# Moving the tiles that two neighbouring blocks share in a gather-and-sum kernel on one Trainium2 core

## The reference

```
x = x + GIN(layernorm(x))          # two sums over edges, four products, relu
x = x + slice_attention(layernorm(x))
x = x + GCN(layernorm(x))          # one sum over edges, weighted by degree
x = x + mixture_of_experts(layernorm(x))   # top 2 of 8 experts
```

## Time and profile before

| | us |
|---|---|
| median of 3 runs | 4030.41 |
| lowest and highest | 4024.98, 4033.82 |
| the profiled execution | 4029.44 |
| its span, first to last instruction | 4027.3 |

### The profile page before, as it was taken

One profiled execution on the slowest core, in us unless ns is written; L12 is line 12 of the kernel. 1 busy time (PEld: TensorE's weight loads), 2 busy tenths in 40 slices (PEclk: granted clock), 3 DMA queues, 4 the chain that ended last, 5 costly groups with the idle time before them and its releaser, 6 DMA issues. The chain is left out here.

```text
span 4027.3 us, 40958 instructions
## 1 busy us (share of the span) xinstructions
PE 3255.7 (81%) x12396; PEld 2172.8 (54%) x12396; DVE 1552.6 (39%) x5917; ACT 496.3 (12%) x1159; POOL 2691.4 (67%) x2719
## 2 busy tenths in 40 slices
PE   3688888888967999999999876567667666769996
PEld 2455555555543555555555464445455554558885
DVE  7422232222213445444444444345454444532221
ACT  3111111111100001010001011000000000023332
POOL 3777777777746777777777403777777777626664
PEclk7899999999988999999999988888888898879998
DMA  6444454444559777777776447444444444438887
GB/s 212 112 130 130 131 149 138 130 130 131 152 154 344 221 219 211 210 215 226 226 212 200 133 139 239 128 141 130 143 132 130 140 130 140 123 111 201 204 202 184
DMA packets 326339, 678.01 MB, mean 168 GB/s; under 512 B 60274, under 2 KB 156886, under 8 KB 325850
## 3 DMA queue, kind: packets, MB, share of 16 engines
q0 software_dynamic: 163376, 455.13, 41.0%
q10 hardware_dynamic: 93460, 117.75, 8.7%
q1 hardware_dynamic: 69290, 102.51, 7.8%
HBM read 582.15 MB, written 100.31 MB: 169 GB/s over the span
## 5 line engine op out<-in xcount | busy, mean ns | idle before, releaser
L292 POOL DMA_INDIRECT s_edge_rows<-table,w_src_idx x2421 | 2383.8, 985 | 796.0 <-issue 704.2
L332 PE MATMUL s_psA<-s_edge_rows,s_onehot 128*128 128x257 f32 (+2 forms) x4626 | 1584.0, 484 | 475.6 <-DMA s_edge_rows<-table,w_src_idx 450.5
L332 PEld LDWEIGHTS s_psA<-s_edge_rows,s_onehot 128*128 128x128 f32 x4626 | 913.3, 205 | 1041.2 <-issue 868.4
L307 DVE TENSOR_SCALAR s_onehot<-w_iota_row,w_dst_l 128x128 f32<-128x128 bf16 x2313 | 494.4, 296 | 16.7 <-PEq L157 15.3
L342 PE MATMUL s_psA<-s_edge_rows,s_early 128*128 128x257 f32 (+2 forms) x864 | 285.6, 461 | 0.0
L2255 POOL DMA_INDIRECT acc_rows<-s_y,s_tnode x105 | 166.2, 1583 | 135.5 <-DVE s_y L2378 110.7
L342 PEld LDWEIGHTS s_psA<-s_edge_rows,s_early 128*128 128x128 f32 x864 | 170.5, 197 | 86.8 <-issue 68.8
L2403 PE MATMUL s_psU<-s_xT,s_w 128*128 128x128 f32 x1680 | 208.0, 278 | 0.2 <-ACT s_xT L2309 0.2
L2413 PE MATMUL s_psD<-moe_w,s_hT 128*128 x840 | 199.6, 381 | 0.0
L2403 PEld LDWEIGHTS s_psU<-s_xT,s_w 128*128 128x128 f32 x1680 | 199.1, 195 | 0.7 <-issue 0.6
L1230 PE MATMUL s_psM<-s_h1T,s_w1b 128*128 128x512 f32 (+2 forms) x448 | 177.6, 542 | 1.6 <-ACT s_h1T L1084 1.6
(11 more groups left out here) (461 smaller groups left out, 2936.3 us busy)
## 6 DMA issues: line engine op xcount, KB each, us to landing
s_w<-in_L_ffn_W_dram SPq DMA_DIRECT2D x105, 512.0 KB, 4.4
s_edge_rows<-table,w_src_idx POOLq DMA_INDIRECT x2421, 2.9
s_swT<-swt_rows SPq DMA_DIRECT2D x12, 1024.0 KB, 7.0
table<-s_trow ACTq DMA_DIRECT2D x11, 1024.0 KB, 4.8
own_rows<-s_own ACTq DMA_DIRECT2D x11, 1024.0 KB, 7.9
s_self_h<-own_rows ACTq DMA_DIRECT2D x11, 1024.0 KB
swt_rows<-s_swT ACTq DMA_DIRECT2D x11, 1024.0 KB, 6.2
extra_rows<-w_zeros SPq DMA_DIRECT2D x7, 896.0 KB, 15.9
```

Source lines behind the costliest of these rows:

```text
L292: pool.indirect_dma_start(self.rows[:, g % self.SLOTS, t, :], None, self.table, bass.IndirectOffsetOnAxis(ap=src_idx[:, at:at + 1], axis=0 ...
L307: last = nc.vector.tensor_scalar(into[:, t, :], iota_row[:, q * P:(q + 1) * P], dst_l[:, at + t:at + t + 1], None, ALU.is_equal)
L332: last = nc.tensor.matmul(banks[b % 2][:, 0:w], self.onehot[:, g % self.AHEAD, t, :], self.rows[:, g % self.SLOTS, t, col:col + w], start= ...
```

## The change

The tile that a block takes early, and the one that its neighbour leaves out, are moved between the third and the fourth block of each unit. The windows become 0 to 16, 15 to 33, 31 to 49 and 48 to 65: 17, 19, 19 and 18 tiles. The groups, the gathers and the unit's 66 tiles stay.

```diff
-UNIT, UT, EARLY, LATE = 4, 66, (0, 3, 5, 4), (1, 2, 0, 0)
+UNIT, UT, EARLY, LATE = 4, 66, (0, 3, 5, 3), (1, 2, 1, 0)
```

## The result

| | us, median | range | runs |
|---|---|---|---|
| before | 4032.67 | 4024.98 to 4033.82 | 5 |
| changed | 4009.94 | 4000.53 to 4011.49 | 5 |

Ratio 0.9947, 95% interval [0.9936, 0.9959]; predicted were 4010.6 us. The profiled execution of the changed kernel took 4010.63 us, its span is 4008.7 us (18.6 less than before) and its mean granted clock 0.924 (before 0.926).

A forecast was written before the change was run, and what follows sets the result against it. TensorE was taken to bound pass 2, the gathers passes 1 and 3. Pass 2's 18.9 us and pass 1's 0.9 sum to 19.8 us less, giving 4010.6 us; own range 4005 to 4017, with rivals 4003 to 4023.

The forecast's parts named there:

- What bounds each pass: All passes: TensorE sets pass 2 (busy 915.6 of 919 us), the gathers set passes 1 and 3.
- Price of a tile: Pass 2: by the spacing of matmuls a tile costs 0.86 us, two tiles 1.72 us a unit.
- Can the gathers follow: Pass 2: gathers keep up with units of 88.3 us, TensorE staying the bound with 0.7 to 1.0 us spare.
- Rival A: Pass 2: the gathers take over, units stop at 89.2 us; 4021 us, at its far end 4029.5; chance 0.11.
- Which units count: Pass 2: unit 0 gives 0, the other 11 units pay in full, 18.9 us; bounds 0 and 20.6.
- Unit 11: Pass 2, last full unit: its two tiles counted in full; were it lost, 1.7 us less.
- rival B: Passes 1 and 3: TensorE waits longer and its clock falls; pass 1's end could add 12 us; chance 0.05.
- Pass 1: Pass 1: only the last full unit's two tiles, in the packed end, pay: 0.9 us; bounds 0 and 0.9.
- Pass 3 and the one-hots: Pass 3 gives 0, at best 0.9 us; VectorE's fewer one-hots give 0, at most 7.1 us a pass.
- C: Whole kernel: unit 0, pass 3 and a little faster gathers pay too; 4005 us; chance 0.06.
- D: Whole kernel: no gain, the saved time comes back in another wait; 4030 us; chance 0.06.
- E: Spare tiles: an edge outside its window forces the fallback to 128, 15 loop turns; 5450 us; chance 0.02.

The follow-up runs named there:

- e10: The changed kernel unaltered, run once more beside the kernel before: 4011.85 us, ratio 0.9955.
- e11: The change in pass 2 alone, passes 1 and 3 as in the kernel before: 4013.95 us, ratio 0.9961 against the kernel before.
- e7: The changed kernel with wider shared windows in pass 2, 81 tiles a unit instead of 73: 4074.88 us, ratio 1.0115 against the kernel before.
- e8: The changed kernel with pass 2's windows of before and some tiles multiplied twice there, 93 a unit: 4196.00 us, ratio 1.0412 against the kernel before.
- e12: The changed kernel with pass 2 cut to 69 tiles a unit, leaving part of the edges out: 4008.23 us, ratio 0.9948 against the kernel before.
- e9: The changed kernel with the windows of before in the first unit of pass 2 alone: 4008.94 us, ratio 0.9951 against the kernel before.
- e3: The changed kernel with VectorE still making the 72 unused one-hots, where before took 4418.33 us: 4422.40 us, ratio 1.0005.
- e5: The changed kernel unaltered, on chips where the kernel before took 4415.17 us: 4421.75 us, ratio 1.0016.

## Why the prediction was right

**The total: right, its closeness partly luck.** Forecast 4010.6 us, measured 4009.94, but the five runs lie 11 us apart. In the profiled run pass 2 gave 14.6 of the 18.9 us predicted, and 4.0 us came elsewhere, where 0.9 were forecast. In e10 and e11 pass 2 gave 18.5 and 18.6 us.

**What bounds each pass: right.** e11 against e10 and the windows of e7, e8 and e12 show it by more and by fewer tiles.

**Price of a tile: right.** Predicted 1.72 us a unit; nine steady units (the third to the eleventh, by TensorE's first edge matmul) took 810.0 us before and 794.3 after, 1.74 each; e10 794.1.

**Can the gathers follow: right, and the spare too.** I gave them 0.7 to 1.0 us a unit to spare at 88.3. The changed kernel itself shows it: in e10 GpSimd still catches up after the late start of pass 2, and for five units it waits for TensorE no longer than the ordinary gap:

```profile
POOL s_edge_rows L292 <- PE s_psA L332: 1.2, 4, 0.3
POOL s_edge_rows L292 <- PE s_psA L342: 0.3, 1, 0.3
```

```profile
1349.30:1786.10 436.80, 336.25 (x330) 1.00 0.75 223
```

336.25 / 330 = 1.019 us a gather, and 436.8 / 5 = 87.4 us a unit; the same stretch of e11 gives 87.6. That is 0.7 to 0.9 us below the 88.3 at which TensorE holds them, of which GpSimd's waits showed 1.1 (forecast 0.7). e12, which drops four tiles more, has units of 87.3 to 88.4, 88.0 in the mean, because its gathers take longer. In its 630 us

```profile
1456.00:2086.00 630.00, 485.74 (x474) 0.99 0.74 223
```

485.74 / 474 = 1.025 us, with the gap 1.330 and 66 of them 87.8 us. The last section tells why: it has other gathers beside VectorE's long instructions. So e12's 88.0 isn't the changed kernel's spare. Rival A, which I priced with units of 89.2 us, hasn't come true.

**Which units count: right in the sum, not in its places.** From the first gather of pass 2 to its last edge matmul it is 1158.0 us before, 1143.3 in the profiled run of the changed kernel, 1139.4 in e10 and 1139.4 in e11: 14.6, 18.5 and 18.6 us less, predicted 18.9. The first two units (predicted 1.7 less together) came out 1.4 us longer, then 2.5 and 1.7 us shorter: they hang on the gathers' start behind the spare edges, which differs from run to run. Unit 11 was counted in full and gave 0.2 us (112.1 to 111.9; 112.1 in e10, 111.8 in e11). That is the step of the working that failed, and TensorE's timeline shows where the 1.5 us went. Before:

```profile
2227.68 1.11 PE L1518 MATMUL s_psT<-w_ident,s_prob 128*128 128x128 f32 x4 [7.25 <-DVE s_prob L1450]
2228.59 2.80 PE L1522 MATMUL s_psM<-s_xl,s_prob 128*128 128x257 f32 x8
2231.23 2.74 PE L332 MATMUL s_psA<-s_edge_rows,s_onehot 128*128 128x512 f32 x6
2233.80 1.88 PE L342 MATMUL s_psA<-s_edge_rows,s_early 128*128 128x512 f32 x4
```

Changed:

```profile
2210.99 1.12 PE L1518 MATMUL s_psT<-w_ident,s_prob 128*128 128x128 f32 x4 [7.26 <-DVE s_prob L1450]
2211.90 3.63 PE L1522 MATMUL s_psM<-s_xl,s_prob 128*128 128x257 f32 x8
2215.33 3.42 PE L332 MATMUL s_psA<-s_edge_rows,s_onehot 128*128 128x512 f32 x6
2218.59 1.88 PE L342 MATMUL s_psA<-s_edge_rows,s_early 128*128 128x512 f32 x4
```

e9:

```profile
2205.48 1.12 PE L1518 MATMUL s_psT<-w_ident,s_prob 128*128 128x128 f32 x4 [7.25 <-DVE s_prob L1450]
...
2212.16 1.88 PE L342 MATMUL s_psA<-s_edge_rows,s_early 128*128 128x512 f32 x4
```

The wait for the softmax is 7.25 or 7.26 us in all three, and the granted clock is down when it ends: windows from 2223.6 to 2230.4 us before, 2206.4 to 2216.7 in the changed kernel and 2202.5 to 2209.3 in e9 show 0.50. But the same 18 matmuls up to the start of the early ones take 6.12 us before, 7.60 after (1.48 more) and 6.68 in e9, because the return to 1.00 comes 2.7, 5.7 and 3.8 us after the wait's end. e10 has 7.78 (0.50 from 2202.1 to 2212.3 us) and no gain in the unit; e9 gains 1.3 us there. It is a loss of rival B's kind, 1.5 us in a place that neither I nor B had looked at: a wait stays as long, and what it costs behind it varies.

**Pass 1: right, as far as one profile can tell.** The last edge matmul comes 1.0 us sooner, counted were 0.9 (four matmuls at 0.217). From the first gather to that matmul the six profiles with the changed windows take 1051.3 to 1053.4 us, the two with the old ones (before and e11) 1053.4 and 1054.3. Another 1.3 us up to pass 2's first gather I hadn't foreseen: before ran a stretch of 3.4 us there at a granted clock of 0.50 (from 1141.6 us) that the changed kernel's trace doesn't have (1.00 from 1136 to 1148 us). That isn't the change's doing. e8 and e12, which have the new windows in pass 1, have such a stretch too (6.7 and 6.8 us at 0.50, from 1139.3 and 1139.5 us) and take 25.6 us from that matmul to the gather (before 24.5); e7, e9, e10 and e11, the last with the old windows, have none (1.00 from 1136 to 1148 us) and take 23.1.

**Pass 3 and the one-hots.** Predicted 0; pass 3 lasts 1049.8 us before and 1048.9, 1053.0 and 1053.3 in the profiled runs of the changed kernel, e10 and e11, so 0.9 us isn't to be told. The one-hots I took as free, with 7.1 us a pass as the bound. They aren't quite: the last section shows gathers that a one-hot holds up, by 16 us in sum over the changed kernel's 2673 one-hots (L307), 6 ns each; by that 72 fewer give 0.4 us in the whole run, an estimate. No run tests it, since e3 ran where nothing could be lost.

**The rivals.** B's clocks are as before (0.94, 1.00, 0.87; after the last gather 0.63, before 0.64; in the last 94 us of pass 1 0.97 in the changed kernel and 0.98 in e10, before 0.98). The range up to 4023 and the chances count B as a loss of some 9 us by the clock, a term that no run shows: the runs showed these clocks, and differences of 1.3 to 1.6 us by the clock at single places, from run to run. Of C's parts only the first unit's gain shows, in e10 and e11; D is refuted by the units; E by the gathers of spare rows (L286), which are 12 in the whole run as before.

## What to carry over

Read for each stretch which engine has no idle time, and price a removed instruction by the spacing of its like in that stretch; elsewhere it brought next to nothing here (0.9955 with passes 1 and 3 changed as well, e10, and 0.9961 without, e11). The spare of the engine next in line is best read where that engine runs free in the same kernel (87.4 us a unit in e10). An experiment that cuts far more than wanted (e12, 88.0) shows that there is a bend, but what the engine collides with is changed in it too. And a gain is the property of a kernel on a chip: where instructions start late, the same edit gave 1.0016 instead of 0.9947.

## What the runs showed of the hardware

**Some gathers end 0.83 us after an instruction of VectorE that was running when they began.** Of the 66 gathers in a steady unit of the changed kernel, 62 or 63 take 0.95 to 1.03 us, at most one more 1.07, and three 2.09, 2.90 and 1.42, always the same three. GpSimd's timeline of the changed kernel:

```profile
1598.25 0.95 POOL L292 DMA_INDIRECT s_edge_rows<-table,w_src_idx  x1 [0.82 <-PE s_psA L332]
1599.51 2.09 POOL L292 DMA_INDIRECT s_edge_rows<-table,w_src_idx  x1 [0.30 <-issue]
...
1605.68 2.90 POOL L292 DMA_INDIRECT s_edge_rows<-table,w_src_idx  x1 [0.30 <-issue]
1608.88 1.42 POOL L292 DMA_INDIRECT s_edge_rows<-table,w_src_idx  x1 [0.30 <-issue]
```

and VectorE's:

```profile
1596.16 2.29 DVE L1443 TENSOR_REDUCE s_gmax<-s_prob 128x32 f32<-128x2048 f32 x1
1598.48 2.29 DVE L1444 TENSOR_TENSOR s_prob<-s_prob,s_gmax 128x2048 f32<-128x2048 f32 x1
...
1605.46 2.29 DVE L1450 TENSOR_TENSOR s_prob<-s_prob,s_gsum 128x2048 f32<-128x2048 f32 x1
...
1608.26 1.22 DVE L1463 TENSOR_TENSOR y_x<-y_x,s_bout 128x1024 f32<-128x1024 f32 x1
```

The three TENSOR_TENSOR end at 1600.77, 1607.75 and 1609.48 us, the three gathers at 1601.60, 1608.58 and 1610.30: 0.82 to 0.83 later each time. The reduction of the same 2.29 us at 1596.16 leaves the gathers beside it at 0.95 us, and so do the sums that read PSUM (L1408, 0.68 us): the 14 gathers that begin during one between 1456 and 2086 us take 0.95 or 0.96 us. A gather that began just before such an instruction isn't held up: the one at 1598.25 takes 0.95 us. Nor is VectorE held up by it: the TENSOR_TENSOR that begins 0.23 us into that gather takes 2.29 us, like the others.

The one-hots (L307) do the same on a smaller scale. The last one of this row of VectorE ends at 543.64 us, and the gather that began during it ends at 544.46, 0.82 later:

```profile
542.97 0.67 DVE L307 TENSOR_SCALAR s_early<-w_iota_row,w_dst_l 128x128 f32<-128x128 bf16 x3
```

```profile
543.40 1.06 POOL L292 DMA_INDIRECT s_edge_rows<-table,w_src_idx  x1 [0.30 <-issue]
```

Of the changed kernel's 2421 gathers 399 begin while a one-hot runs, and 209 of these take more than 0.97 us. That is 0.02 to 0.12 us each, but for one, and 16 us in sum.

So the cost depends on how the gathers stand to VectorE's work. In e10's five free units the gather under L1444 takes 2.19, 3.05, 3.04, 2.19 and 1.90 us, and the units take 87.1, 88.0, 88.0, 87.0 and 86.8. In e12 one under L1422 comes on top, with 1.16 to 1.95 us (before had it in its steady units too, mostly with 1.40), where those five of e10 have at most 1.03. That is what makes e12's gathers slower (1.025 us in the mean, 1.019 in those units of e10). What makes a gather wait for VectorE's instruction isn't shown; the rows give only which gathers do, and for how long. I read all this from the traces and tested it in no experiment.

**One kernel, two speeds of start.** On two chips all kernels took 4413 to 4427 us instead of 4009 to 4030, with starts late on several engines (a register move of 29 ns taking up to 699 ns) and the durations on VectorE, ScalarE and GpSimd unchanged (e5 750, 384 and 962 ns for L1179, L1076 and the mean of GpSimd's in pass 1; before 751, 383 and 964).
